# Turning nine of x's quantized tiles on VectorE inside the attention units, with GpSimd taking low parts

## The chip, the cores and the metric

The kernel runs on one core of a Trainium2 chip. The metric is the device time of one execution in microseconds (us): the median of the runs. A profiled execution has a span, from the first to the last instruction of the core, and a time of its own a little above it; the runs have no trace.

Engine names in the rows: PE is TensorE's matmuls, PEld its weight loads, DVE is VectorE, ACT is ScalarE, POOL is GpSimd, SPq the queue from which SyncE issues transfers. ps is PSUM.

## The reference, cut to what matters

The sizes are B = 4, T = 512, D = 512, 32 heads of 16, one key and one value head shared by all heads, and a feed-forward block of 2048 features.

```python
xn = layernorm(x)
s = attention(xn, wq, wk, wv, wo)        # causal; k and v are shared by the 32 heads
h = linear8bit(xn, W1, b1)
g = silu(linear8bit(h, W2, b2))
out = x + s * g

def linear8bit(x, W, b):
    col_max = max(abs(x)) over all rows
    outlier = col_max > 3.0
    y = quant_rows(where(outlier, 0, x)) @ quant_rows(W).T
    return y + where(outlier, x, 0) @ W.T + b
```

quant_rows rounds each row to multiples of its largest absolute value / 127.

## The kernel before, in words

The 2048 rows of x are 16 tiles of 128 rows. The kernel has three stages. The first normalizes x, stores it to DRAM and makes queries, keys and values. The second is attention. The third is the feed-forward block, whose first layer multiplies W1 by the quantized x, which has to lie in SBUF turned: the feature on the partition, the token along the row. Two big tensors hold it, big_h (the part that TensorE's fast format keeps) and big_l (what is left). Until then the same two tensors hold the queries and then the attended rows: tile i of x may be written only once the rows of tile i have been projected.

**Attention** runs over 16 units (4 batches by 4 groups of 8 heads). A unit has 24 steps, and all engines run the same list of steps `g`, each with its own part of each step in a fixed order. Parts that belong to different units are shifted against each other (the exponentials of a unit run 35 steps behind the start of its maxima). In a step there are, on PE: one piece of the raw scores for the row maxima (`max_piece`, L1010, into one of three PSUM banks `MAXB`), one piece of the final scores (L1023, three banks), in some steps the product with the values (`pv`, L1036) or one k of a row tile's output projection (L1061 to L1063: three matmuls, four k for each of 16 row tiles). On VectorE: the maximum of the piece (L933), which frees its bank; PE may not write piece n before the maximum of piece n - 3 is taken. In some steps there are also transposes and reciprocals of the normalization (L900 to L914) and the quantization of one tile of x (L723, L727, L731, L734). On ScalarE: the exponential (L854), the high part of the attended rows (L859), evictions (L715, L871) and the last step of quantization (L864). On GpSimd: the causal mask after some exponentials (L836), the inlier product and the rounding for x (L804, L809) and the low part of the attended rows (L825). SyncE's queue stores the quantized tile `xm` to `xe_scratch` in DRAM (L763, one transfer of 128 rows of 2 KB), loads the next normalized tile (L759), the queries of a later unit (L161, 12 transfers of 64 KB) and the maxima (L749), and stores projected rows (L789). GpSimd's product for tile u + 1 overwrites `xm` and waits for the store of tile u (`s_xes`).

Counted within a unit (g modulo 24), GpSimd has a mask in steps 1, 5, 7, 8, 14, 18, 20 and 21 and the product L804 in step 2. Of the products with the values, the one that uses the masks of steps 1 and 5 stands in step 9.

**The turned x before.** The first 12 tiles (`EARLY`) are turned once the last maximum piece is done (g = 384): every second step from g = 385 on, PE transposes a tile loaded back from DRAM (four 128 by 128 transposes with the identity, L1097, into a bank of `MAXB`), a step later ScalarE copies the high part into big_h (L881), and a step later VectorE subtracts to get the low part (L947). The loads (L769) go through two buffers and wait for the transposes two tiles back. In the same steps stand the exponentials, masks and value products of the last two units and the projection of the third batch's last three row tiles. The projection of the fourth batch follows at g = 423, and the feed-forward stage after that. The last four tiles are turned there and are not touched.

## Time and profile before

| | |
|---|---|
| median of 3 runs | 789.14 us (788.95 to 1225.57) |
| the profiled execution: its time | 788.52 us |
| its span | 786.8 us |
| mean granted TensorE clock | 0.984 |
| busy: PE, DVE, ACT, POOL | 752.1 (96%), 651.5 (83%), 396.0 (50%), 273.6 us (35%) |
| attention's steps g = 0 to 383, until | 364.1 us of the span |
| first matmul of the feed-forward stage | 409.09 us |
| a step block of 24 without projection / with it | 17.5 / 18.28 us |

Busy time of PE is that of matmuls with modelled ends: they are pipelined, so that one of 512 columns lasts 0.39 us and the next starts 0.23 us after it. A row of a timeline gives start and duration, both in us, then engine, line and operation, output and inputs, and how many such instructions are merged in it. The distance from one start to the next is what an instruction takes from its engine when it is kept busy.

The 24-step blocks can be told by L936, which ends each of them on VectorE: at 163.44, 180.94, 199.56, 217.84, 236.12, 254.40, 272.68, 290.97, 309.25, 327.54, 345.82 and 364.10 us. Blocks are numbered from 0 by g // 24; block 10 begins at 254.4 us.

### The profile page before, as it was taken

What the parts mean: (1) busy time and instruction counts of PE and PEld (TensorE: products, weight loads), DVE (VectorE), ACT (ScalarE), POOL (GpSimd) and SP (SyncE); (2) the same over time, 40 slices, a digit from 0 to 9 for tenths busy, and PEclk for the clock granted to TensorE, in tenths of its full rate; (3) what the DMA queues carried; (4) which work ended last, traced back from release to release, by engine and by line L of the source; (5) the groups of instructions that cost most, each with busy time, mean ns of one, the idle gap of its engine ahead of it and who ended that gap; (6) DMA issues with size and microseconds to landing.
All of it is one profiled execution on the core that took longest, in us unless ns stands there. A gap on an engine that the chain in (4) does not pass through costs nothing. (4 is left out here: it accounts for less than half of the span.)

```text
span 786.8 us, 11983 instructions
## 1 busy us (share of the span) xinstructions
PE 752.1 (96%) x4133; PEld 567.0 (72%) x4133; DVE 651.5 (83%) x1116; ACT 396.0 (50%) x671; POOL 273.6 (35%) x349
## 2 busy tenths in 40 slices
PE   5999899999999999999999999999997999999995
PEld 4877575556666677666568878878886888888884
DVE  7988989999989999987447668597859998599957
ACT  4454066676777677667824445355554333132212
POOL 7213135555555555555442112122100000027404
PEclk9999689999999999999999999999999999999998
DMA  7431302332333332233455677646334678427982
GB/s 261 157 108 54 78 21 70 86 83 76 91 91 105 89 83 84 83 83 122 135 192 185 166 237 197 202 105 161 88 62 131 240 241 255 157 87 245 332 278 107
DMA packets 93772, 110.71 MB, mean 141 GB/s; under 512 B 43136, under 2 KB 50320, under 8 KB 92176
## 3 DMA queue, kind: packets, MB, share of 16 engines
q1 hardware_dynamic: 93712, 109.95, 45.8%
q8 instruction: 33, 0.54, 0.3%
q14 instruction: 27, 0.22, 0.1%
HBM read 56.43 MB, written 40.37 MB: 123 GB/s over the span
## 5 line engine op out<-in xcount | busy, mean ns | idle before, releaser
L933 DVE TENSOR_REDUCE rowmax<-ps 128x2 f32<-128x512 f32 (+3 forms) x384 | 210.7, 590 | 20.3 <-PE ps L1010 18.7
L854 ACT ACTIVATE probs<-ps 128x512 f32<-128x512 f32 (+1 forms) x352 | 175.3, 557 | 72.0 <-PE ps L1023 70.3
L1010 PE MATMUL ps<-km,stack 128*128 128x256 f32 (+3 forms) x512 | 150.2, 347 | 2.6 <-PEq L195 1.9
L1023 PE MATMUL ps<-stack,ks 128*128 128x512 f32 (+1 forms) x352 | 132.8, 387 | 2.7 <-ACT probs L854 2.7
L1010 PEld LDWEIGHTS ps<-km,stack 128*128 128x128 f32 (+1 forms) x512 | 95.1, 199 | 43.1 <-DVE rowmax L933 23.5
L836 POOL TENSOR_SCALAR_AFFINE_SELECT probs<-probs 128x512 f32<-128x512 f32 x128 | 81.0, 641 | 78.9 <-ACT probs L854 77.3
L1880 PE MATMUL ps<-big_h 128*128 128x512 f32 x256 | 100.0, 390 | 2.0 <-DVE big_l L1696 1.6
L1881 PE MATMUL ps<-big_l,big_h 128*128 128x512 f32 x256 | 99.6, 389 | 0.0
L1882 PE MATMUL ps<-big_h,big_l 128*128 128x512 f32 x256 | 99.6, 389 | 0.0
L1036 PE MATMUL ps<-probs,vones 128*32 128x512 f32 (+3 forms) x1024 | 82.2, 439 | 0.2 <-POOL probs L836 0.2
L1023 PEld LDWEIGHTS ps<-stack,ks 128*128 128x128 f32 x352 | 67.4, 192 | 11.7 <-ACT probs L854 6.2
L1880 PEld LDWEIGHTS ps<-big_h 128*128 128x128 f32 x256 | 48.0, 188 | 12.6 <-issue 2.6
L1036 PEld LDWEIGHTS ps<-probs,vones 128*32 128x32 f32 x1024 | 26.7, 109 | 41.2 <-issue 28.1
L1882 PEld LDWEIGHTS ps<-big_h,big_l 128*128 128x128 f32 x256 | 48.1, 188 | 10.1
L1881 PEld LDWEIGHTS ps<-big_l,big_h 128*128 128x128 f32 x256 | 48.1, 188 | 9.7
L1625 DVE TENSOR_TENSOR absmax<-absmax,habs 128x2048 f32<-128x2048 f32 x15 | 34.3, 2285 | 22.0 <-ACT habs L1265 22.0
L1857 PE MATMUL ps<-big_h,w_high_first 128*128 128x512 f32 x128 | 50.8, 397 | 1.6 <-PEq L708 1.6
L1857 PE MATMUL ps<-big_h,w_high_second 128*128 128x512 f32 x128 | 50.7, 396 | 1.4 <-POOL w_low_second L1427 1.4
L1546 ACT CAST big_h<-habs 128x1024 fp32r<-128x1024 f32 x31 | 32.4, 1045 | 39.0 <-DVE habs L1668 23.3
L1859 PE MATMUL ps<-big_h,w_low_second 128*128 128x512 f32 x128 | 50.5, 395 | 0.0
L1859 PE MATMUL ps<-big_h,w_low_first 128*128 128x512 f32 x128 | 50.5, 395 | 0.0
L1858 PE MATMUL ps<-big_l,w_high_first 128*128 128x512 f32 x128 | 50.5, 395 | 0.0
(227 smaller groups left out, 1370.0 us busy)
## 6 DMA issues: line engine op xcount, KB each, us to landing
stack<-big_h SPq DMA_DIRECT2D x128, 64.0 KB, 2.0
h_scratch<-hs SPq DMA_DIRECT2D x7, 1024.0 KB, 4.7
hload<-h_scratch SPq DMA_DIRECT2D x14, 512.0 KB, 5.2
xn_scratch<-xa SPq DMA_DIRECT2D x4, 1024.0 KB, 4.4
stack<-big_l SPq DMA_DIRECT2D x64, 64.0 KB, 2.0
xi<-xn_scratch SPq DMA_DIRECT2D x16, 256.0 KB, 2.7
xe_scratch<-xm SPq DMA_DIRECT2D x16, 256.0 KB, 2.3
w2n<-in_L_ffn_W_dram SPq DMA_DIRECT2D x4, 1024.0 KB, 6.5
```

What stands on the lines that cost most here:

```text
L836: nc.gpsimd.affine_select(out=d, in_=d, compare_op=ALU.is_ge, fill=0.0, base=0, pattern=[[0, NPAIR], [1, P]], channel_multiplier=-1).then_ ...
L854: nc.scalar.activation(probs[p][:, o:o + nh * w], ps[:, STB[n % NST], 0:nh * w], ACT.Exp).then_inc(s_exp, 1)
L933: nc.vector.tensor_reduce(dst, src, AX_X, ALU.max).then_inc(s_red, 1)
L1010: last = nc.tensor.matmul(dst, stack[u % 3][rows, hp, P * qt:P * (qt + 1)], km[rows, u // KT, p0:p0 + npar, keys], start=True, stop=True)
L1023: ins = nc.tensor.matmul(ps[:, STB[n % NST], 0:nh * w].rearrange("p (h q) -> p h q", h=nh), ks[:, u // KT, p, P * kt:P * (kt + 1)], stack[ ...
L1036: ins = nc.tensor.matmul(ps[32 * j:32 * j + 32, PVB, P * kt:T], vones[:, u // KT, kt, :], probs[p][:, o:o + w], start=(kt == 0), stop=(kt ...
L1857: nc.tensor.matmul(dst, w1h[f % 2][:, k, :], big_h[:, k, t], start=(k == 0), stop=False)
L1858: nc.tensor.matmul(dst, w1h[f % 2][:, k, :], big_l[:, k, t], start=False, stop=False)
L1859: last = nc.tensor.matmul(dst, w1l[f % 2][:, k, :], big_h[:, k, t], start=False, stop=(k == KT - 1))
L1880: nc.tensor.matmul(ps[:, i, :], hqh[m % RB][:, t], w2h[m % RB], start=(kk == 0), stop=False)
L1881: nc.tensor.matmul(ps[:, i, :], hqh[m % RB][:, t], w2l[m % RB], start=False, stop=False)
L1882: return nc.tensor.matmul(ps[:, i, :], hql[m % RB][:, t], w2h[m % RB], start=False, stop=(kk == FT - 1))
```

## The change

Nine tiles (0 to 8, `STEADY`) are turned within the blocks 7 to 15, one in each, in step 2 of the block; tiles 9, 10 and 11 at g = 386, 394 and 402. VectorE turns a tile in SBUF, in blocks of 32 by 32, with one instruction. For that to be the whole transpose, the first 12 tiles are stored to DRAM with their 32 by 32 blocks exchanged: four transfers of 32 partitions each, whose pieces in DRAM are 32 elements (128 bytes). The load back is issued 19 steps before the turn, in step 7 of the block before, and it comes into `tail_rows[:, 0]`; the turned tile stands in `tail_rows[:, 1]`. One step after the turn ScalarE copies it to big_h, now from SBUF, and two steps after it GpSimd (not VectorE) subtracts for big_l. PE's 48 transposes are gone. The next turn on VectorE waits for GpSimd's subtraction of the tile before. The wait for big_l's 12 tiles and for the last maximum moves to the projection of the fourth batch.

```diff
         EARLY = NT - QT
-        TAIL_STEP = 2
+        def x_stores(n):
+            return 16 * (HB * min(n, EARLY) + max(n - EARLY, 0))
         W1_LOAD_AT, W1_SCALE_AT, W1_ROUND_AT = 21, 30, 31
         W2_LOAD_AT, W2_SCALE_AT = 28, 38
         W1_TURN_AT, W1_HIGH_AT, W1_LOW_AT = 36, 37, 37
...
         def projected_rows(i):
             return tail_rows[:, i % 2, :] if i in TAIL_OUT else ob[:, i % 2, :]
-        def tail_tile(g, after=0):
-            i, r = divmod(g - after - CH * U - 1, TAIL_STEP)
-            return i if r == 0 and 0 <= i < EARLY else -1
+        TURN_AT, STEADY = 2, 9
+        def turned(g, after=0):
+            t = g - after
+            if t < CH * U:
+                i = t // CH - KT - 3
+                return i if t % CH == TURN_AT and 0 <= i < STEADY else -1
+            i, r = divmod(t - CH * U - TURN_AT, 8)
+            return STEADY + i if r == 0 and i < EARLY - STEADY else -1
+        def x_fetched(g):
+            i = turned(g, 5 - CH)
+            if 0 <= i <= STEADY:
+                return i
+            i = turned(g, -6)
+            return i if i > STEADY else -1
         misc = []
         for g in range(STEPS):
...
                     u = unit_at(g, XSTORE_AT)
                     if u >= 0:
                         sp.wait_ge(s_xe, u + 1)
-                        sp.dma_start(xe_d[P * u:P * (u + 1), :], xm[:, :]).then_inc(s_xes, 16)
-                    i = tail_tile(g, -5)
+                        if u < EARLY:
+                            for b in range(HB):
+                                sp.dma_start(xe_d[P * u:P * (u + 1), :]
+                                             .rearrange("(a j) (k b i) -> b j k a i", a=HB, k=KT, b=HB)[b],
+                                             xm[SQ * b:SQ * (b + 1), :].rearrange("j (k a i) -> j k a i", k=KT, a=HB)
+                                             ).then_inc(s_xes, 16)
+                        else:
+                            sp.dma_start(xe_d[P * u:P * (u + 1), :], xm[:, :]).then_inc(s_xes, 16)
+                    i = x_fetched(g)
                     if i >= 0:
-                        sp.wait_ge(s_xes, 16 * (i + 1))
-                        if i >= 2:
-                            sp.wait_ge(s_tt, i - 1)
-                        sp.dma_start(tail_rows[:, i % 2, :], xe_d[P * i:P * (i + 1), :]).then_inc(s_tr[i % 2], 16)
+                        sp.wait_ge(s_xes, x_stores(i + 1))
+                        if i:
+                            sp.wait_ge(s_tt, i)
+                        sp.dma_start(tail_rows[:, 0, :], xe_d[P * i:P * (i + 1), :]).then_inc(s_tr, 16)
                     if unit_at(g, XSTORE_AT + 1) == U - 1:
                         sp.wait_ge(s_xm, NT)
-                        sp.wait_ge(s_xes, 16 * (EARLY + 1))
+                        sp.wait_ge(s_xes, x_stores(EARLY + 1))
                         sp.dma_start(inlier_row[:, :], xe_d[P * EARLY:P * (EARLY + 1), :]).then_inc(s_xel[0], 16)
                     if unit_at(g, W1_LOAD_AT) == U - 1:
                         sp.wait_ge(s_xt, NT)
...
                     if u >= 0:
                         pool.wait_ge(s_xl, 16 * (u + 1))
                         if u:
-                            pool.wait_ge(s_xes, 16 * u)
+                            pool.wait_ge(s_xes, x_stores(u))
                         nc.gpsimd.tensor_tensor(xm[:, :], xi[:, :], inlier_row[:, :],
                                                 ALU.mult).then_inc(s_xm, 1)
                     u = unit_at(g, XROUND_AT)
...
                         pool.wait_ge(s_ah, u + 1)
                         nc.gpsimd.tensor_tensor(attended(big_l, u), tb[:, :, :].rearrange("p a b -> p (a b)"),
                                                 attended(big_h, u).bitcast(F32), ALU.subtract).then_inc(s_al, 1)
+                    i = turned(g, 2)
+                    if i >= 0:
+                        pool.wait_ge(s_xh, i + 1)
+                        nc.gpsimd.tensor_tensor(big_l[:, :, P * i:P * (i + 1)],
+                                                tail_rows[:, 1, :].rearrange("p (k t) -> p k t", k=KT),
+                                                big_h[:, :, P * i:P * (i + 1)].bitcast(F32),
+                                                ALU.subtract).then_inc(s_xlo, 1)
                     u, s_ = scored(g)
                     p, i = divmod(s_, NB)
                     if u >= 0 and s_ < 2 * NB and i + 1 in KT_END:
...
                     b, j, k = projected(g, 1)
                     if b >= 0 and k == KT - 1:
                         evict(act, b, j)
-                    i = tail_tile(g, 1)
+                    i = turned(g, 1)
                     if i >= 0:
+                        act.wait_ge(s_mf, misc_at[("o", *divmod(i, QT))] + 1)
                         act.wait_ge(s_tt, i + 1)
                         nc.scalar.copy(big_h[:, :, P * i:P * (i + 1)],
-                                       ps[:, MAXB[i % NMAX], :].rearrange("p (k t) -> p k t", k=KT)).then_inc(s_xh, 1)
+                                       tail_rows[:, 1, :].rearrange("p (k t) -> p k t", k=KT)).then_inc(s_xh, 1)
             @block.vector
             def _(dve):
...
                     for part in range(4):
                         if unit_at(g, XSCALE_AT + part) >= 0:
                             quantize_x(dve, unit_at(g, XSCALE_AT + part), part)
-                    i = tail_tile(g, 2)
+                    i = turned(g)
                     if i >= 0:
-                        dve.wait_ge(s_xh, i + 1)
-                        nc.vector.tensor_tensor(big_l[:, :, P * i:P * (i + 1)],
-                                                ps[:, MAXB[i % NMAX], :].rearrange("p (k t) -> p k t", k=KT),
-                                                big_h[:, :, P * i:P * (i + 1)].bitcast(F32),
-                                                ALU.subtract).then_inc(s_xlo, 1)
+                        dve.wait_ge(s_tr, 16 * (i + 1))
+                        if i:
+                            dve.wait_ge(s_xlo, i)
+                        nc.vector.transpose(tail_rows[:, 1, :], tail_rows[:, 0, :]).then_inc(s_tt, 1)
                     if unit_at(g, W1_SCALE_AT) == U - 1:
                         dve.wait_ge(s_w1n[0], 16)
...
                     if k == 0:
                         misc_bank(("o", b, j))
                         if b == B - 1 and j == 1:
+                            pe.wait_ge(s_red, CH * U)
                             pe.wait_ge(s_xlo, EARLY)
                     pe.wait_ge(s_al, KT * b + k + 1)
                     c = slice(P * j, P * (j + 1))
...
                         maxima(maximized(g, MAX_AT))
                     if projected(g)[0] >= 0:
                         project(*projected(g))
-                    i = tail_tile(g)
-                    if i >= 0:
-                        pe.wait_ge(s_tr[i % 2], 16 * (i // 2 + 1))
-                        if i < NMAX:
-                            pe.wait_ge(s_red, CH * U)
-                        else:
-                            pe.wait_ge(s_xlo, i - NMAX + 1)
-                        for k in range(KT):
-                            last = nc.tensor.transpose(ps[:, MAXB[i % NMAX], P * k:P * (k + 1)],
-                                                       tail_rows[:, i % 2, P * k:P * (k + 1)], ident[:, :])
-                        last.then_inc(s_tt, 1)
                     if unit_at(g, W1_TURN_AT) == U - 1:
                         pe.wait_ge(s_w1r, 1)
                         pe.wait_ge(s_exp, 2 * NB * U)
```

## Rows read from the trace of the kernel before

**Rows 1.** Page, part 1: busy us, share of the span, instructions of each engine.
```profile
PE 752.1 (96%) x4133; PEld 567.0 (72%) x4133; DVE 651.5 (83%) x1116; ACT 396.0 (50%) x671; POOL 273.6 (35%) x349
```

**Rows 2.** Windows: two blocks and the stretch after the last; per engine busy (count).
```profile
146.40:163.90 17.50, 16.88 (x123) 10.24 (x122) 16.86 (x37) 12.14 (x26) 9.92 (x14) 1.00 0.29 79
218.00:236.30 18.30, 18.30 (x136) 12.67 (x135) 16.78 (x38) 12.92 (x28) 10.00 (x14) 1.00 0.32 89
364.30:409.10 44.80, 40.38 (x270) 26.81 (x270) 21.87 (x40) 28.00 (x56) 19.92 (x25) 1.00 0.44 144
```

**Rows 3.** Timeline of DVE in block 10 (one answer per narrow window).
```profile
255.28 3.27 DVE L933 TENSOR_REDUCE rowmax<-ps 128x2 f32<-128x512 f32 x6
...
256.48 0.68 DVE L933 TENSOR_REDUCE rowmax<-ps 128x4 f32<-128x512 f32 x1
257.19 0.56 DVE L933 TENSOR_REDUCE rowmax<-ps 128x1 f32<-128x384 f32 x1
...
262.09 0.56 DVE L933 TENSOR_REDUCE rowmax<-ps 128x1 f32<-128x384 f32 x1 [0.50 <-PE ps L1010]
...
269.50 0.70 DVE L914 STREAM_TRANSPOSE tb<-ta 128x512 f32<-128x512 f32 x1
270.13 0.65 DVE L933 TENSOR_REDUCE rowmax<-ps 128x4 f32<-128x512 f32 x1
```

**Rows 4.** Timeline of PE in block 10.
```profile
257.17 0.34 PE L1010 MATMUL ps<-km,stack 96*128 96x384 f32 x1
...
257.52 0.28 PE L1010 MATMUL ps<-km,stack 128*128 128x256 f32 x1
...
257.87 0.44 PE L1010 MATMUL ps<-km,stack 96*128 96x256 f32 x2
...
259.97 1.71 PE L1036 MATMUL ps<-probs,vones 128*32 128x512 f32 x16
```

**Rows 5.** Timelines of DVE and of PE in an earlier block, without projection.
```profile
141.50 0.43 DVE L933 TENSOR_REDUCE rowmax<-ps 128x2 f32<-128x256 f32 x1
141.98 0.39 PE L1010 MATMUL ps<-km,stack 128*128 128x256 f32 x1
```

**Rows 6.** Timelines of POOL and of the SP queue in block 10.
```profile
257.43 1.30 POOL L804 TENSOR_TENSOR xm<-xi,inlier_row 128x512 f32<-128x512 f32 x1 [1.10 <-DMA xe_scratch<-xm]
258.77 0.64 POOL L836 TENSOR_SCALAR_AFFINE_SELECT probs<-probs 128x512 f32<-128x512 f32 x1
...
253.48 0.58 SPq L763 DMA_DIRECT2D xe_scratch<-xm  x1
```

**Rows 7.** Stores of a like shape: page, part 6, and line L1304 (duration ns min/median/max).
```profile
w2t_scratch<-w2e SPq DMA_DIRECT2D x64, 64.0 KB, 2.0
L1304 SPq DMA_DIRECT2D w2t_scratch<-w2e x64: 303/503/1292, 426.4 to 575.3; - x64
```

**Rows 8.** PE's transposes: lines (busy, mean ns), timeline, and a wait of 364:409.
```profile
L1097 PE MATMUL ps<-ident,tail_rows 128*128 128x128 f32 x48 | 7.4, 278 | 0.8 <-DMA tail_rows<-xe_scratch 0.7
...
370.87 0.60 PE L1097 MATMUL ps<-ident,tail_rows 128*128 128x128 f32 x4
371.22 0.47 PE L1023 MATMUL ps<-stack,ks 128*128 128x512 f32 x1
...
PE ps L1097 <- DMA tail_rows<-xe_scratch: 0.7, 1, 0.7
```

**Rows 9.** Timelines of ACT, POOL and PE near the end of the last unit.
```profile
385.94 0.63 ACT L859 CAST big_h<-tb 128x512 fp32r<-128x512 f32 x1
...
386.65 1.29 POOL L825 TENSOR_TENSOR big_l<-tb,big_h 128x512 fp32r<-128x512 f32 x1 [2.87 <-ACT big_h L859]
387.88 1.23 POOL L836 TENSOR_SCALAR_AFFINE_SELECT probs<-probs 128x512 f32<-128x512 f32 x2
390.91 0.64 POOL L836 TENSOR_SCALAR_AFFINE_SELECT probs<-probs 128x512 f32<-128x512 f32 x1 [1.79 <-ACT probs L854]
...
390.29 0.86 PE L1036 MATMUL ps<-probs,vones 128*32 128x256 f32 x16
```

More of the change, by code:

```diff
@@ L551, in block_layernorm_attention_ffn @@
         rec = sa("rec", [P, 2, T // 32])
+        HB, SQ = 4, 32
         def attended(part, u):
@@ L607, in block_layernorm_attention_ffn @@
         s_nm = sem("heads_divided")
-        s_tr = [sem(f"tail_rows_loaded{i}") for i in range(2)]
-        s_tt = sem("tail_rows_transposed")
+        s_tr = sem("x_blocks_loaded")
+        s_tt = sem("x_blocks_turned")
         s_w1n = [sem(f"w1_loaded{i}") for i in range(2)]
@@ L790, in _ @@
                                      ).then_inc(s_obt if n in TAIL_OUT else s_obs[n % 2], 16)
-                sp.wait_ge(s_xes, 16 * NT)
+                sp.wait_ge(s_xes, x_stores(NT))
             @block.gpsimd
@@ L1154, in block_layernorm_attention_ffn @@
         s_t2 = sem("absmax_transposed")
-        HB, SQ = 4, 32
         def w2_pieces(f):
```

## The prediction

> **What bounds the kernel now.** I read the page's busy shares first, then the windows by block, then the timelines of single blocks, last the stretch after g = 383. PE is busy 96% of the span [rows 1]; the reader should not stop there, because the change touches only the attention stage. There two kinds of block are to be told apart. Without projection a block takes 17.5 us, with 16.88 us of PE and 16.86 of DVE [rows 2]: PE and DVE take turns at waiting for each other. With projection it takes 18.28 us, PE is busy throughout and DVE 16.78 [rows 2]. So the blocks in which the nine turns are put are bound by PE, and DVE has about 1.5 us left in each. That room is an average. What counts is where in the block it lies, since PE may not write a piece before DVE has taken the maximum three pieces back. After the last block follow 44.8 us in which PE is busy 40.38 [rows 2], with the 48 transposes among them.
>
> **The blocks: the turn on DVE.** No row shows this instruction, but L914 is the same operation on the same shape from SBUF to SBUF: it lasts 0.70 us, and the next maximum starts 0.63 us after it [rows 3]. I take 0.63; below, an idle engine would make it 0, above, 0.70. It comes behind the third maximum. In block 10 the maxima of steps 1 to 6 stand without a gap to speak of [rows 3]; that of step 3 starts at 256.48 and ends at 257.16, that of step 4 starts at 257.19, some 0.1 us later than it could, since it waits for PE. With the turn the one ends at 257.79 and the other, with 0.53 of delay left, at 257.75 + 0.53 = 258.28.
> PE's piece of step 6 needs the first of these, that of step 7 the second. They start now at 257.52 and 257.87 [rows 4]. How soon PE follows a maximum is seen in an earlier block: a maximum ends at 141.93 and PE's piece starts at 141.98 [rows 5]. So step 6 starts at 257.84 (0.32 late) and step 7 at 258.33, 0.46 late, and 0.45 is what I take. The piece of step 10 isn't late on DVE's account: before its maximum DVE idles 0.50 us [rows 3], which swallows the 0.53. From there DVE is again where PE puts it. Nothing gives PE's 0.45 us back, since it has no idle time in such a block. It has the same margins in each of blocks 7 to 15: 9 x 0.45 = **+4.05 us**. Bounds: 9 x 0 if the piece of step 7 isn't really held, and 9 x 0.70 = 6.3 if the whole turn lands on PE.
>
> **The blocks: what stands beside.** ScalarE's copy waits for the turn to end at 257.18; it and what is behind it (the exponential of step 4, the eviction L871, then PE's projection) come about 0.4 us late, no later than PE. It is free while PE sets the pace; without PE's delay it would cost the same 0.4, not in addition. The load back is a unit ahead and costs one issue on a queue that waits in that place.
> The store becomes four transfers of 64 KB in pieces of 128 bytes. The same shape is stored at L1304: 0.50 us of issue, 2.0 from issue to landing [rows 7]. Issued from 253.48 on [rows 6], 0.54 apart, the last lands at 253.48 + 1.62 + 2.0 = 257.1. GpSimd's product L804 waits for it and starts now at 257.43, released by the single store [rows 6]; so nothing gets later. The three more issues (1.6 us) push the store of projected rows back, and SP waits idle after that.
> GpSimd's subtraction costs 1.29 us (L825, the same operation [rows 9]). It comes behind L804, and behind it are the masks of steps 5, 7 and 8. L804 ends at 258.7, the subtraction at 259.95, the mask of step 5 at 260.6. PE's value product starts at 259.97 [rows 4] and reaches the half that needs this mask about 0.9 later, 261.3 with PE's own delay. Margin 0.7 us: I cost it at nothing, and its price if the cover is gone is the time by which L804 starts after 258.2.
> The Trainium skill (DMA: Bandwidth & Descriptors, Why small descriptors are slow) speaks against such a store: each packet carries a fixed 3 cycles over its 32-byte beats, 7 instead of 4 for 128 bytes. L1304's transfers agree in so far as 64 KB land in 2.0 us: the cost is there but below a microsecond. By the rule alone the sum would stay, as long as the last transfer lands by 258.2.
>
> **The stretch after the blocks.** PE loses twelve groups of four transposes. Four start at 370.87 and the next matmul at 371.22 [rows 8]: 0.35 us, 0.35 to 0.42 over the twelve, together 4.5. The wait for a loaded tile, 0.7 [rows 8], goes too: 5.2 us at most. Two things stand in the way. One group (g = 395) lies in the shadow of an eviction that PE waits for, 0.36 lost. The larger is GpSimd, which must now do tile 11's subtraction in g = 404, behind L825 and ahead of the masks of g = 404 and 405. L825 follows ScalarE's L859, 385.94 [rows 9]. Up to there ScalarE gains 1.9 us from the five groups before g = 394 and, from g = 395 on, three copies fewer at 0.5 (five of the old go, two of the new come): 3.4, less the shadowed 0.36, so L825 starts at 386.65 - 3.05 = 383.6. It ends at 384.8, the subtraction at 386.05, the masks at 386.65 and 387.25. PE has its value product of g = 411 at 390.29 [rows 9]; it could start at 385.2 but its second half waits for the last mask until 387.3, where it began at 390.7: 3.4 us earlier instead of 5.1. After that the masks at 390.91 and later [rows 9] come 3.7 earlier and set the last value products. I take **-3.7 us**, bounds -3.0 and -5.2. The projection and the start of the feed-forward stage shift with it, and that stage is PE's own: nothing there is bought or lost.
>
> **The sum**, against the profiled 788.52: + 4.05 - 3.7 = 788.9. The median of the runs lies 0.6 above the profiled time; a part of that I add: **789.3 us**.
>
> **The rivals.**
> *A, the forecast*: the turn costs PE what DVE lacks, the stretch returns it. 787 to 791.5. Chance 0.55.
> *C, the turns are absorbed*: PE isn't held in steps 6 and 7, and the 1.5 us of DVE's room cover 0.63. For it: DVE's idle share. Against it: the margins at 257.52 and 257.87 are 0.36 and 0.13 us. It gives 788.5 - 3.7 + 0.5 = 785.3. Chance 0.17.
> *B, GpSimd's queue becomes the bound in the blocks*, the case on the slower side: the last of the four stores lands late, L804 starts after 258.2, the subtraction stands before the mask of step 5, and PE waits for it in step 9. For it: the single store of block 10 took 3.95 us to release L804 (253.48 to 257.43 [rows 6]), twice what L1304's take. A last landing 4.0 after its issue (259.1) costs 0.9 in each of the 8 blocks 7 to 14: 789.3 + 7.2 = 796.5. Against it: today the store of projected rows is issued right behind and shares the engines, in future only after. Chance 0.24, of it 0.03 that the store lands 2.0 us beyond the threshold or more, from where on it decides over 2% (8 x 2.0 = 16).
> *D, the transposes count in full*, so that moving them is worth more than their distance: 7.4 us busy [rows 8] and the wait 0.7, minus 4.05, gives 785.1, and with C 781. Against it: they overlap. Chance 0.04.
> Under the rule of the Trainium skill (VectorE: DVE Perf Modes, The three transpose paths) a 128 by 128 transpose costs TensorE 390 ns, 48 of them 18.7 us, so by it D would give some 774; the trace has four in 0.35 us, which is against it.
>
> **How the numbers follow.** The likeliest case is A. The range takes in C at its low end and the lower half of B: 785.0 to 795.0; outside are the rest of B (0.11) and most of D (0.04) and some of C (0.03). About 2%, 15.8 us, is what a measurement of this kernel can tell from no change. Faster by that much takes more than C and D together: 0.01. Slower needs B beyond its threshold: 0.03. Within 2%: 0.96.
>
> **What would show it.** Blocks 7 to 15 of 18.7 us instead of 18.28, with the whole difference between PE's pieces of steps 5 and 8, prove the DVE step right; 18.3 proves C. PE waiting for L836 in step 9, with L804 released by the store, is B. In the stretch, PE waiting at the value product of g = 411 for a mask behind the new subtraction supports -3.7; if the feed-forward stage starts 5 us earlier after block 15's end than now, the GpSimd step was wrong. The prediction falls if stores of 128 bytes behave otherwise beside 12 query loads than L1304's, or if the exponentials of ScalarE, not GpSimd, set the stretch.

## The result and the profile after

| | before | after |
|---|---|---|
| median, 8 runs each | 789.3 us (788.7 to 1225.57) | 794.87 us (791.02 to 797.05) |
| ratio of the two | | 1.0068 [1.0047, 1.009] |
| profiled execution: its time, its span | 788.52, 786.8 | 791.02, 789.2 |
| blocks 7 to 15 in the profile | 164.5 | 171.4 |
| end of block 15 to the feed-forward stage | 45.0 | 41.7 |

One execution of before lies at 1225.57 us, far from all others, and plays no part. The forecast was 789.3, with a range of 785.0 to 795.0; the change costs 0.7%. The profiled execution is the lowest of the eight, so what it shows is the least that the change did.

What follows rests on the lengths of the blocks, from one start of the block-ending maximum to the next. Before, each of blocks 7 to 15 takes 18.28 us. After:

```
block       7      8      9      10     11     12     13     14     15
after     18.72  18.70  18.70  19.57  19.01  19.49  19.28  19.20  18.69
```

Two levels are to be seen: 18.7 in four blocks, and up to 0.9 more in the five from 10 to 14. The sum is 6.8 us more than before; the stretch after the blocks gives 3.3 back, what lies ahead of block 7 is 1.6 shorter in this execution and the feed-forward stage 0.4 longer: 6.8 - 3.3 - 1.6 + 0.4 = 2.3, and the spans differ by 2.4. The last two are no effect of the change that the runs show: in the traces of this document the part ahead of block 7 takes 196.9 to 199.6 us (199.6 in before, 197.9 in a run with the same code up to there), and the feed-forward stage 377.7 to 379.7, once 382.1.

The changed kernel's page, part 1: busy us, share of the span, instructions.

```profile
PE 749.4 (95%) x4085; PEld 560.3 (71%) x4085; DVE 649.0 (82%) x1116; ACT 396.1 (50%) x671; POOL 288.6 (37%) x361
```

Beside [rows 1], PE has its 48 transposes less, and GpSimd twelve subtractions more, 15.0 us. PE is no longer busy throughout in the blocks. Its waits by releaser over 180 to 412 us (sum, count, longest):

```profile
PE ps L1070 <- POOL probs L870: 3.1, 5, 1.3
PE ps L1044 <- DVE rowmax L968: 1.9, 9, 0.2
```

L870 is what L836 was (the mask), L968 what L933 was (the maximum), L1044 and L1070 are the pieces and the value product, L831 is the product that was L804. Nine waits for a maximum, one for each of the nine blocks; of the five for a mask, the longest lies in the stretch and four in the blocks (in block 11, the fifth that loses time, it is PE's weight load that waits for the mask). The timeline of DVE in block 10 of after, which begins at 254.10 (first columns start and duration), and then that of PE:

```profile
254.97 1.28 DVE L968 TENSOR_REDUCE rowmax<-ps 128x2 f32<-128x512 f32 x2
256.17 0.70 DVE L984 STREAM_TRANSPOSE tail_rows<-tail_rows 128x512 f32<-128x512 f32 x1
256.80 1.91 DVE L968 TENSOR_REDUCE rowmax<-ps 128x4 f32<-128x512 f32 x4
```

```profile
257.05 0.33 PE L1057 MATMUL ps<-stack,ks 128*128 128x384 f32 x1
257.59 0.36 PE L1044 MATMUL ps<-km,stack 128*128 128x256 f32 x1 [0.21 <-DVE rowmax L968]
...
258.02 0.45 PE L1044 MATMUL ps<-km,stack 96*128 96x256 f32 x2
...
260.07 1.06 PE L1070 MATMUL ps<-probs,vones 128*32 128x512 f32 x8
261.79 0.85 PE L1070 MATMUL ps<-probs,vones 128*32 128x384 f32 x8 [0.65 <-POOL probs L870]
```

The turn takes its engine for 0.63 us. Counted from the start of the block, PE's piece of step 6 starts at 3.49 instead of 3.12 [rows 4], that of step 7 at 3.92 instead of 3.47: 0.37 and 0.45 late, where 0.32 and 0.46 were forecast. Then the value product comes in two parts with a hole of 0.65 us between them (0.86 by the starts, since eight take 0.86 and the second part starts 1.72 after the first), where before all 16 ran together [rows 4]. That hole is the second level. GpSimd's timeline, and the issues of SP's queue in the same block:

```profile
258.59 1.31 POOL L831 TENSOR_TENSOR xm<-xi,inlier_row 128x512 f32<-128x512 f32 x1 [2.57 <-DMA xe_scratch<-xm]
259.85 1.30 POOL L857 TENSOR_TENSOR big_l<-tail_rows,big_h 128x512 fp32r<-128x512 f32 x1
261.08 1.83 POOL L870 TENSOR_SCALAR_AFFINE_SELECT probs<-probs 128x512 f32<-128x512 f32 x3
```

```profile
253.69 3.17 SPq L785 DMA_DIRECT2D xe_scratch<-xm  x4
```

The chain is complete in these four rows: the four stores take 3.2 us of SP's queue, GpSimd waits 2.57 us for the last to land, starts L831 at 258.59, does the new subtraction behind it, and only then the mask for which PE stands still. Block 8, where nothing is lost, and block 14, where 0.5 is:

```profile
215.84 2.65 SPq L785 DMA_DIRECT2D xe_scratch<-xm  x4
...
331.20 2.63 SPq L785 DMA_DIRECT2D xe_scratch<-xm  x4
```

These last as long as each other, but the first begins 0.86 before its block (216.70) and the second 0.25 before (331.45). For all nine blocks, in us from the start of the block: the issue of the first and of the last of the four, the start of L831, and by how much the block is over 18.7 (block 15 has one plain store):

```
block       7     8     9     10    11    12    13    14    15
first     -0.86 -0.86 -0.87 -0.41 -0.87  0.00 -0.34 -0.25  0.28
last       1.14  1.15  1.13  2.12  1.55  2.01  1.67  1.76   -
L831      3.51  3.52  3.51  4.49  3.95  4.44  4.22  4.13  2.70
over 18.7  0     0     0    0.87  0.31  0.79  0.58  0.50   0
```

In each of the five the loss is the start of L831 less 3.62 to 3.65; the prediction put that point at 258.2 - 254.4 = 3.8. And L831 follows the last issue by 2.37 in five of the eight blocks with four stores, by 2.40 to 2.56 in the others. So the landing is steady; what varies is when the last issue happens: either the whole row begins late, behind the query loads of the same queue (blocks 12 to 14), or a single store in it takes long (block 11), or both (block 10).

In the stretch, the timelines of GpSimd and PE (block 15 ends at 369.34):

```profile
388.93 1.27 POOL L852 TENSOR_TENSOR big_l<-tb,big_h 128x512 fp32r<-128x512 f32 x1 [2.69 <-ACT big_h L893]
390.17 1.27 POOL L857 TENSOR_TENSOR big_l<-tail_rows,big_h 128x512 fp32r<-128x512 f32 x1
391.39 1.80 POOL L870 TENSOR_SCALAR_AFFINE_SELECT probs<-probs 128x512 f32<-128x512 f32 x3
```

```profile
392.07 1.01 PE L1070 MATMUL ps<-probs,vones 128*32 128x256 f32 x16 [1.26 <-POOL probs L870]
```

PE does wait for the masks behind tile 11's subtraction. Its value product starts 22.73 us after block 15, against 26.19 before [rows 9]: 3.46 us earlier. The 3.3 us of the stretch are one draw: the five other traces in which GpSimd subtracts tiles 9 to 11 have 41.6 to 42.7 us there, so it gave 2.3 to 3.4.

### The profile page after: what moved, and what is told of

Its sections match the earlier page's. It is cut to its first block and busy times, and to the rows that moved or that the text cites. A ratio compares the mean times of both kernels' runs of the same rounds, so it can differ in the third digit from the quotient of the medians.

```text
span 789.2 us, 11946 instructions
## 1 busy us (share of the span) xinstructions
PE 749.4 (95%) x4085; PEld 560.3 (71%) x4085; DVE 649.0 (82%) x1116; ACT 396.1 (50%) x671; POOL 288.6 (37%) x361
## 5 line engine op out<-in xcount | busy, mean ns | idle before, releaser
L968 DVE TENSOR_REDUCE rowmax<-ps 128x2 f32<-128x512 f32 (+3 forms) x384 | 210.3, 590 | 22.7 <-PE ps L1044 21.2
L1044 PE MATMUL ps<-km,stack 128*128 128x256 f32 (+3 forms) x512 | 150.6, 347 | 4.6 <-DVE rowmax L968 2.4
L1044 PEld LDWEIGHTS ps<-km,stack 128*128 128x128 f32 (+1 forms) x512 | 94.1, 197 | 48.4 <-DVE rowmax L968 23.1
L870 POOL TENSOR_SCALAR_AFFINE_SELECT probs<-probs 128x512 f32<-128x512 f32 x128 | 80.0, 642 | 54.0 <-ACT probs L888 53.9
L1070 PE MATMUL ps<-probs,vones 128*32 128x512 f32 (+3 forms) x1024 | 83.5, 439 | 3.4 <-POOL probs L870 3.1
L1070 PEld LDWEIGHTS ps<-probs,vones 128*32 128x32 f32 x1024 | 26.0, 109 | 46.7 <-issue 24.7
L1880 PE MATMUL ps<-big_l,w_high_second 128*128 128x512 f32 x128 | 50.5, 395 | 0.0
```

The source lines that it names most:

```text
L870: nc.gpsimd.affine_select(out=d, in_=d, compare_op=ALU.is_ge, fill=0.0, base=0, pattern=[[0, NPAIR], [1, P]], channel_multiplier=-1).then_ ...
L968: nc.vector.tensor_reduce(dst, src, AX_X, ALU.max).then_inc(s_red, 1)
L1044: last = nc.tensor.matmul(dst, stack[u % 3][rows, hp, P * qt:P * (qt + 1)], km[rows, u // KT, p0:p0 + npar, keys], start=True, stop=True)
L1070: ins = nc.tensor.matmul(ps[32 * j:32 * j + 32, PVB, P * kt:T], vones[:, u // KT, kt, :], probs[p][:, o:o + w], start=(kt == 0), stop=(kt ...
L1880: nc.tensor.matmul(dst, w1h[f % 2][:, k, :], big_l[:, k, t], start=False, stop=False)
```

## The experiments

The theory after the result is that two separate costs add up, 0.42 us in each of nine blocks from the turn on VectorE and the rest from the stores in four parts, through GpSimd. The first two experiments undo the second cost in two ways, the third brings in the first cost by itself. The median of before is given anew with each experiment, 788.1 to 788.9 us; a ratio is always to the before beside it.

**The store in one part.** It leaves out the exchange of the 32 by 32 blocks.

```diff
-            return 16 * (HB * min(n, EARLY) + max(n - EARLY, 0))
+            return 16 * n
...
-                        if u < EARLY:
+                        if u < 0:
```

> The changed kernel, but each of the first 12 tiles is stored with the one transfer of 2 KB rows again, so x's blocks lie in the wrong order (that part of the result is left out). Theory (PE loses 0.43 us per block to the turn, and in blocks 10 to 14 another 0.3 to 0.85 because the last of four stores releases GpSimd's product L804 late and its subtraction then stands before the mask that PE needs): blocks 7 to 15 all take 18.7 us, GpSimd's product starts 1.9 to 3.0 us into a block, no value product waits for a mask; 791.0 - 3.0 = 788 us, ratio to before about 0.999. Rival (the subtraction on GpSimd costs this by itself, whatever the store does): blocks 10 to 14 stay at 19.0 to 19.6, ratio 1.007. Rival (the traffic of loads back disturbs): as the second.

Measured: 789.26 us, 1.0002 [0.9985, 1.0019] of before (788.88). All nine blocks take 18.7, together 3.8 us more than before. GpSimd's timeline in its block 10, from 255.17 on:

```profile
257.49 1.29 POOL L831 TENSOR_TENSOR xm<-xi,inlier_row 128x512 f32<-128x512 f32 x1 [0.40 <-DMA xe_scratch<-xm]
258.75 1.29 POOL L857 TENSOR_TENSOR big_l<-tail_rows,big_h 128x512 fp32r<-128x512 f32 x1
```

L831 starts 2.3 after the block instead of 4.5, and PE waits for no mask in the blocks. The second level is gone, the first has stayed.

**The subtraction behind the masks** (in step 9 of the block instead of step 4; tiles 9 to 11 as they were). The stores stay in four parts.

```diff
                     # GpSimd, ahead of the subtraction of the nine tiles
-                    i = turned(g, 2)
+                    i = turned(g, 7)
... (for tiles 9 to 11 turned(g, 2), as it was)
```

> The changed kernel, with GpSimd's nine subtractions of the blocks moved from step 4 to step 9, behind the masks of steps 5, 7 and 8. Theory: the store may land as late as now, but nothing that PE needs stands behind the subtraction: blocks 7 to 15 take 18.7 us, ratio about 0.999. Rival (a late L804 alone delays the mask of step 5 and VectorE's L723): blocks 10 to 14 stay over 18.9, ratio 1.003 or more.

Measured: 789.2 us, 0.9998 [0.9984, 1.0012]. Blocks of 18.68 to 18.73. GpSimd in block 10 (from 254.64):

```profile
259.46 1.30 POOL L831 TENSOR_TENSOR xm<-xi,inlier_row 128x512 f32<-128x512 f32 x1 [2.89 <-DMA xe_scratch<-xm]
260.69 1.82 POOL L874 TENSOR_SCALAR_AFFINE_SELECT probs<-probs 128x512 f32<-128x512 f32 x3
262.47 1.30 POOL L861 TENSOR_TENSOR big_l<-tail_rows,big_h 128x512 fp32r<-128x512 f32 x1
```

Here the product starts 4.8 after the block, later than in any block of after, and nothing is lost. So a late store alone costs nothing, and the subtraction ahead of the masks alone costs nothing (previous run); only both together do.

**The turn alone, in the kernel before.** Nine turns of a row that is there anyway; nothing else of the change.

```diff
+                    if g < CH * U and g % CH == 2 and g // CH >= 7:
+                        nc.vector.transpose(tail_rows[:, 1, :], magic_row[:, :])
```

> The kernel before with nine more 128x512 transposes on VectorE in step 2 of blocks 7 to 15 (from a constant row into a buffer that nobody reads there), nothing else. Theory: each delays PE's pieces of steps 6 and 7 and costs 0.43 us, blocks 7 to 15 at 18.7, all of them alike: 789.3 + 3.9 = 793.2 us, ratio 1.005. Rival (the cost of blocks 7 to 9 comes from ScalarE's copy ahead of the exponential and the eviction): 18.28 us a block, ratio 1.000.

Measured: 792.93 us against 788.88, +4.05 us, 1.0048 [1.003, 1.0067]. Blocks of 18.64 to 18.69, 3.44 together. DVE and PE in block 8 (216.31 to 234.99), then the block as a window (length; PE, PEld, DVE, ACT and POOL busy; clock; DMA share; GB/s):

```profile
218.67 0.70 DVE L945 STREAM_TRANSPOSE tail_rows<-magic_row 128x512 f32<-128x512 f32 x1
...
220.09 0.36 PE L1012 MATMUL ps<-km,stack 128*128 128x256 f32 x1 [0.24 <-DVE rowmax L933]
...
216.31:234.99 18.68, 18.44 (x135) 12.61 (x135) 17.25 (x38) 12.89 (x27) 9.98 (x14) 1.00 0.31 87
```

The same wait of PE at the same piece as in after: of the 0.42 us a block of the first level, 0.38 are the turn on VectorE by itself. Where the other 0.04 come from isn't shown; ScalarE's copy is one candidate. DVE is idle for 1.4 of 18.7 us in this block, and that does not help: its idle time lies elsewhere in the block.

**The turn in another place.** In step 22 of the block before DVE waits for PE ahead of a maximum. Only the turn and what counts from it move.

```diff
-                i = t // CH - KT - 3
-                return i if t % CH == TURN_AT and 0 <= i < STEADY else -1
+                i = t // CH - KT - 2
+                return i if t % CH == BLOCK_TURN_AT and 0 <= i < STEADY else -1   # 22
```

> The changed kernel, with the nine turns in step 22 of the block before instead of step 2 (the copy in step 23, the subtraction in step 0). VectorE idles 0.85 us there today, and GpSimd is idle before the mask of step 1. Theory: both costs go, the blocks with a turn take 18.3 us, and with the 3.3 us that the stretch after the blocks gives the kernel takes 785.5 to 786.5, ratio 0.996. Rival (the turn costs PE 0.4 us wherever it stands, as DVE has no room): 18.7 us a block, ratio 0.999 to 1.001.

Measured: 790.13 us, 1.0014 [1.0001, 1.0026], blocks of 18.75 to 18.79: no better than in step 2, and the theory of this run failed. DVE around the turn, then ScalarE and PE:

```profile
215.78 0.69 DVE L984 STREAM_TRANSPOSE tail_rows<-tail_rows 128x512 f32<-128x512 f32 x1
216.72 0.56 DVE L968 TENSOR_REDUCE rowmax<-ps 128x1 f32<-128x384 f32 x1 [0.25 <-PE ps L1044]
...
217.45 0.61 ACT L916 CAST big_h<-tail_rows 128x512 fp32r<-128x512 f32 x1
217.96 1.85 ACT L888 ACTIVATE probs<-ps 128x512 f32<-128x512 f32 x4
...
218.61 0.44 PE L1057 MATMUL ps<-stack,ks 128*128 128x384 f32 x1 [0.22 <-ACT probs L888]
```

The turn itself became free: after it DVE still waits 0.25 for PE. But ScalarE's copy moved with it, to step 23, where the exponentials are not ahead of PE: they come 0.5 late and PE waits for one. A new wait took the place of the old one. The next run gives every part its own place.

**Three parts, three idle places.** As in the last run, with ScalarE's copy in step 9 and GpSimd's subtraction in step 10 of the next block.

```diff
+        def behind(g, in_block, later):
+            i = turned(g, in_block)
+            if 0 <= i < STEADY:
+                return i
+            i = turned(g, later)
+            return i if i >= STEADY else -1
...
-                    i = turned(g, 2)        # GpSimd's subtraction
+                    i = behind(g, 12, 2)
...
-                    i = turned(g, 1)        # ScalarE's copy
+                    i = behind(g, 11, 1)
```

> The changed kernel with the nine turns in step 22 of the block before, as in the run with step 22, but ScalarE's copy in step 9 and GpSimd's subtraction in step 10 of the block after the turn, where each of them idles. In the run with step 22 alone VectorE's maxima were as before and PE waited in step 3 for an exponential that stood behind the copy. Theory (the cost is whichever engine's order the part stands in, not the work): blocks 6 to 15 at 18.3 us, against 18.77; with 3.3 us from the stretch after the blocks the kernel takes 785.5 to 786 (ratio 0.996). Rival (the blocks have no room for the three parts at all): 18.6 or more.

Measured: 785.95 us against 788.9, 0.9963 [0.995, 0.9977]. Blocks: 18.28 to 18.32 in seven of nine, 18.45 and 18.48 in blocks 12 and 14; +0.4 in all. A block as a window (columns as above):

```profile
216.59:234.87 18.28, 18.28 (x136) 12.66 (x135) 17.37 (x38) 13.40 (x28) 11.15 (x15) 1.00 0.43 103
```

DVE is busy 17.37 us in it, more than in after (17.24 in block 8), and the block has before's length. Two blocks still lose 0.2: there the product on GpSimd starts 4.6 and 4.7 after the block, lasts 1.3, and delays the mask of step 5 to 5.9 without any subtraction between.

**The later tiles, too.** As above, and the subtractions of tiles 9, 10 and 11 by VectorE again.

```diff
                     # GpSimd
-                    if i >= 0:
+                    if 0 <= i < STEADY:
...
                     # VectorE, ahead of the turn
+                    i = turned(g, 2)
+                    if i >= STEADY:
+                        dve.wait_ge(s_xh, i + 1)
+                        nc.vector.tensor_tensor(big_l[...], tail_rows[:, 1, :], big_h[...], ALU.subtract)
```

> The run before this one, and tiles 9, 10 and 11 are subtracted by VectorE two steps after their turn instead of by GpSimd. Theory (in the stretch after the blocks PE waits 1.3 us for masks that stand behind GpSimd's subtraction of tile 11): that wait goes, the stretch shrinks from 41.7 to about 40.4 us, total 784.5, ratio 0.994. Rival (ScalarE's exponentials set that stretch, and the mask is late only as far as they are): the stretch keeps 41.5 us.

Measured: 785.68 us, 0.9953 [0.9935, 0.997]. The stretch takes 40.38 us instead of 42.1, and its GpSimd and PE show why:

```profile
383.91 1.28 POOL L860 TENSOR_TENSOR big_l<-tb,big_h 128x512 fp32r<-128x512 f32 x1 [2.68 <-ACT big_h L901]
385.14 1.80 POOL L878 TENSOR_SCALAR_AFFINE_SELECT probs<-probs 128x512 f32<-128x512 f32 x3
...
385.82 1.01 PE L1085 MATMUL ps<-probs,vones 128*32 128x256 f32 x16
```

The masks follow L860 at once, and PE's product has no wait. Yet the median is only 0.3 below the run before and 1.2 above the 784.5 of the theory. In the profiled execution the span is even 0.3 longer than in the run before: of the 1.8 us gained, 0.4 is given back in blocks with late stores, 0.7 ahead of block 7 and 1.0 in a longer feed-forward stage (378.9 against 377.9). This run by itself does not prove that the gain in the stretch reaches the end.

**The turn in step 2 once more,** copy in step 3, subtraction in step 9, VectorE's subtractions for tiles 9 to 11: against the last run only the places in the blocks differ, those of the turn, of the copy and of the subtraction.

> The changed kernel with the nine subtractions in step 9 as in the run with that alone, and tiles 9, 10 and 11 subtracted by VectorE. Blocks 7 to 15 stay at 18.70 us. Theory: the stretch takes about 40.3 us against 41.6, ratio 0.998. Rival: 41.5 us, ratio 1.000.

Measured: 787.54 us, 0.9989 [0.9976, 1.0002], blocks of 18.70, 3.8 together against 0.8 in the last run, stretch 40.38 again. Moving the three parts to their idle places is worth 3.0 us in the blocks and 1.9 in the medians.

**Ten tiles in the blocks** instead of nine (`STEADY = 10`; tiles 10 and 11 stay at g = 394 and 402), otherwise as in the last but one.

> As the run with free slots and VectorE's subtractions, but tile 9 too is turned in step 22 of block 15, tiles 10 and 11 after the blocks. Theory: PE does not transpose either of them, so one tile more or less in the stretch changes nothing that sets its end: within 0.3 us of that run. Rival (each tile in the stretch costs ScalarE 0.5 us there, and ScalarE sets it): 0.5 us less.

Measured: 785.83 us, 0.9951 [0.9931, 0.9972], stretch 40.39. The tenth tile moves nothing: once no mask waits behind a subtraction, no tile in the stretch is in PE's way. What PE still waits for there are exponentials, two evictions (1.03 and 0.94 us) and the start of the feed-forward stage (1.62). In this execution block 10 took 19.14 and block 11 18.75; in them GpSimd's product starts 5.32 and 4.94 after the block, behind stores of which the first took 2 us to issue. So the improved places don't do away with the late store; the last two runs do.

**The changed kernel again, and two stores.** Three runs are left: the changed kernel itself once more, then the improved one (places as above, nine tiles, VectorE's subtractions) with the store in one part, which again leaves out the exchange, and last the improved one with the four stores in another place of SP's queue, behind the first six query loads of a later unit instead of behind all twelve.

> The changed kernel as it is, once more. Theory (the last of four stores lands at a time that differs from execution to execution, and where it is late PE waits for the mask behind GpSimd's subtraction): blocks 7 to 9 again 18.70, blocks 10 to 14 again between 18.9 and 20, but not the same numbers as in the first profile; total between 791 and 797. Rival (the loss of blocks 10 to 14 belongs to something fixed in the program): the same block lengths to 0.1 us.

Measured: 794.36 us against 788.14, 1.0081 [1.0064, 1.0099]. Its blocks sum to 9.3 us over before, after's to 6.8; blocks 8 and 10 are the long ones now (19.83 and 20.33). The stores of its block 10 (from 254.21) and GpSimd behind them, then the same of block 8 (from 215.64):

```profile
253.91 3.87 SPq L785 DMA_DIRECT2D xe_scratch<-xm  x4
...
259.52 1.29 POOL L831 TENSOR_TENSOR xm<-xi,inlier_row 128x512 f32<-128x512 f32 x1 [3.38 <-DMA xe_scratch<-xm]
...
214.78 2.63 SPq L785 DMA_DIRECT2D xe_scratch<-xm  x4
...
220.46 1.29 POOL L831 TENSOR_TENSOR xm<-xi,inlier_row 128x512 f32<-128x512 f32 x1 [2.89 <-DMA xe_scratch<-xm]
```

In block 10 one store took 1.85 us to issue, and L831 follows the last issue by the usual 2.37. In block 8 the issues were early and short, and for once the landing was late: 3.68 after the last issue. The expectation failed in these two blocks (8 was to stay at 18.70, 10 below 20).

Nor is all of the loss a matter of chance. Over 18.7, blocks 12 to 14 lose 0.85, 0.51 and 0.51 here and 0.79, 0.58 and 0.50 in after, the same to 0.1 us, as the rival said. Of the four stores in block 10 one is long in both (after, then this run), and the same query load ahead of block 14 is:

```profile
254.35 1.15 SPq L785 DMA_DIRECT2D xe_scratch<-xm  x1
326.77 1.22 SPq L161 DMA_DIRECT2D stack<-big_h  x1
...
253.91 1.85 SPq L785 DMA_DIRECT2D xe_scratch<-xm  x1
328.12 1.31 SPq L161 DMA_DIRECT2D stack<-big_h  x1
```

Counted in the order of SP's issues over the whole trace, this holds for all nine traces with four stores (632 issues each): in the blocks from 10 on there are six places, the 205th or 206th issue, the 225th to 227th, the 243rd or 244th, the 260th to 263rd, the 279th and the 293rd or 294th, and in 51 of the 54 cases the issue there takes 0.97 to 2.04 us. With the stores in their old place, the first two places fall on the four stores of blocks 10 and 11 and the others on query loads ahead of blocks 12 to 15; in blocks 7 to 9 only the run with the stores between the query loads (the last one below) has issues of such a length, two of them. So the place is nearly fixed by the order of the queue, and what changes between executions is the length, most of all in blocks 10 and 11.

> The run with free slots and VectorE's subtractions after the blocks, but with one plain transfer for each stored tile (x's blocks in the wrong order, that part of the result is left out). Theory: what blocks 10, 12 and 13 of that run lost (18.45 to 18.57) is the late landing of four stores: all blocks 7 to 15 at 18.28 to 18.3, 0.7 us less in all, ratio 0.994. Rival (the loads back or the subtraction cause it): unchanged.

Measured: 784.34 us, 0.995 [0.9936, 0.9964]; all nine blocks 18.28 to 18.31. The 0.2 to 0.3 left in single blocks was the store's.

```diff
                     # SP, in the step of the query loads
-                        queries(u + 3)
+                        queries(u + 3, range(0, 2))
+                        store_x(u)
+                        queries(u + 3, range(2, NPAIR))
... (the old place keeps the stores of the last three units alone)
```

> The run with free slots and VectorE's subtractions, correct in full, with the four stores of a tile issued between the first six and the last six loads of the queries instead of behind all twelve. Theory: the last store then lands before the next block begins, GpSimd's product L831 starts 1.9 us into every block and no longer when the store allows, blocks 7 to 15 at 18.28, ratio 0.994. Rival (the later six loads of queries come too late for PE, or the queue waits for ScalarE's last step of quantization): 18.5 or more.

Measured: 783.6 us (783.3 to 784.76), 0.9943 [0.9929, 0.9958]. SP in block 9, and GpSimd in block 10 (from 252.74):

```profile
248.29 2.64 SPq L777 DMA_DIRECT2D xe_scratch<-xm  x4
...
254.02 0.64 POOL L883 TENSOR_SCALAR_AFFINE_SELECT probs<-probs 128x512 f32<-128x512 f32 x1 [0.58 <-ACT probs L901]
254.62 1.28 POOL L844 TENSOR_TENSOR xm<-xi,inlier_row 128x512 f32<-128x512 f32 x1
```

The product starts 1.9 after the block in every block and waits for nothing; blocks of 18.28 to 18.33. The long issues stand at the same places of the queue, but now the stores have time for them: the 205th issue is a query load now (1.54 us at 252.29), and where a store is the long one (the 279th, 1.61 us, block 14) the product still starts at 1.9. This version computes everything and is faster than both kernels: 4.5 us below the before beside it, some 11 below after. Against the version with late stores (0.9953) its profile has 0.7 us less in the blocks; the intervals of the two ratios overlap, so the medians alone don't show that step.

## Why the prediction was right and wrong

**The turn on DVE: right, in size and place.** +4.05 was forecast (0.45 a block), and 3.8 are in the blocks of the runs without the second cost (0.42 a block); the turn alone in the kernel before costs 3.4 in the blocks and 4.05 in the median. It came from following two maxima to the two pieces that wait for them. The share of idle time (rival C) would have given nothing; C is refuted by the blocks of 18.7.

**The stretch: right in its cause, a little too large.** -3.7 was forecast, -3.3 measured in after and -2.3 to -3.4 over the six traces with this code, against a bound of -3.0; the cause is the named one: the value product of g = 411 waits for a mask behind tile 11's subtraction and starts 3.46 us earlier (forecast 3.4). L852 follows block 15 by 19.59; the prediction had 383.6 - 364.1 = 19.5. With the subtraction on VectorE the stretch takes 40.38, 4.6 less than before. Rival D is refuted as well: the most that the stretch returned is 4.6, not 8.1. (The 390 ns for one transpose in the prediction are the figure of the Trainium skill, VectorE: DVE Perf Modes, The three transpose paths, for bf16; the transposes here are fp32, and [rows 8] has four in 0.35 us.)

**The store: the step that failed.** "Issued from 253.48 on [rows 6], 0.54 apart, the last lands at 253.48 + 1.62 + 2.0 = 257.1 ... so nothing gets later." The term was put at nothing and cost 3.05 us in the profiled execution, 5 to 6 by the medians. The mechanism was that of rival B; two terms of this sum were too small and one was read in one block only. Line L785 of after (duration ns min/median/max):

```profile
L785 SPq DMA_DIRECT2D xe_scratch<-xm x48: 616/629/1154, 126.6 to 333.2; - x48
...
DMA to landing us min/median/max: 2.2/2.2/3.2
```

First, the sizes: an issue takes 0.63, not 0.50 [rows 7], the next follows at 0.67, and GpSimd follows the last issue by 2.37, not 2.0. That makes 3 x 0.67 + 2.37 = 4.38 instead of 3.62. From 0.92 before the block, as in block 10 of before, L831 starts at 3.46: still ahead of the threshold, and just what blocks 7 to 9 show (3.51, nothing lost). The margin was 0.2, not 0.7.

Second, the place: 253.48 was taken from block 10 and applied to all. The trace of before has the store as early as that in blocks 7 to 11 alone; in blocks 12 to 14 it is issued 0.44, 0.70 and 0.17 before the block. SP's queue in before ahead of block 14 (327.54), and GpSimd behind it:

```profile
322.80 1.35 SPq L161 DMA_DIRECT2D stack<-big_h  x1
...
327.36 0.58 SPq L763 DMA_DIRECT2D xe_scratch<-xm  x1
...
329.81 1.29 POOL L804 TENSOR_TENSOR xm<-xi,inlier_row 128x512 f32<-128x512 f32 x1 [0.35 <-DMA xe_scratch<-xm]
```

One of the twelve query loads took 1.35 us to issue instead of 0.59, and the store behind them was late by as much. Before, that cost nothing; with 4.38 behind it, -0.17 becomes 4.21 and 0.58 us of loss (0.50 measured in after). By this way the three blocks give 0.3, 0.05 and 0.6, about 1 us together that could be read in the trace of before. Block 11 could be read too: right behind its single store the next issue, of projected rows, takes 1.11 us there. With one of the four stores in that place the sum is -0.92 + 4.38 + 0.48 = 3.94, a loss of 0.3, and 0.31 is measured. Block 10 has no long issue in before, but 1.04 to 2.12 us at this place in the three other traces with single stores; its 0.87, and how long each long issue gets, no single trace could give. The prediction had the spread in its rows, 303 to 1292 ns [rows 7] and the 3.95 us of the single store [rows 6], and held its margin against the median.

**The sum.** By the medians, the changed kernel without the second cost is at 789.2 (subtraction moved) and 789.26 (store in one part), which is the forecast of 789.3; the second cost is the 5 to 6 us that are left. B came on top of A, as its price of 796.5 had it, in five of the eight blocks and not in all. The most likely case, A with 787 to 791.5, did not come. That 794.87 lies within the range is owed to the half of B that was taken into it, and by 0.13 us to luck: four of the eight executions lie above 795.0. The 0.4 us added for median over profile were too little, 3.85 measured, for the same reason: where a cost depends on how long a queue's issues get, one profile is a draw. That after's other seven executions, up to 797.05, lose their time in the same place is inferred from the second profile of the program (2.5 us more in the blocks, span 2.2 longer); they were not traced. The two runs in which the store can cost nothing have their profiled time near or above the median (789.3 to 789.2, 790.59 to 789.26).

**The small packets.** The Trainium skill (DMA: Bandwidth & Descriptors, Why small descriptors are slow) speaks of a fixed cost for each small packet in the engines. The landing of 64 KB in 128-byte pieces at 2.2 us agrees in so far as that cost can't be more than a part of 2.2 us. No run here shows the cost itself, so the prediction's "the cost is there" was not read from a row: the plain store of 256 KB landed in 2.3 us. What the four stores added was time in the issuing queue, three more issues, 3 x 0.67 = 2.0 us.

## What to carry to other kernels

- An instruction moved to another engine is costed at its place in that engine's order, by following its successors to the first one on which the bound engine waits; the same three parts cost 0.42 us a block in one set of places, 0.5 in another and nothing in a third, where VectorE was no less busy. Every part needs its own place: when the copy moved along behind the turn, one wait was only exchanged for another.
- A margin behind a DMA is to be held against the latest issue of all its instances, not one, and against the upper end of the row. Long issues are to be looked for by their place in the queue: a transfer that is put in such a place, or behind it, takes the delay over. Four transfers for one add three issues to the queue; the cure was to issue them earlier, between other transfers of the same queue.

## What the runs showed of the hardware

- An issue of 64 KB in 512 pieces of 128 bytes takes SP's queue 0.63 us (0.616 to 0.64 in nearly all), but single issues on that queue, query loads as well as stores, take 0.97 to 2.04. In the nine traces with four stores they come in blocks 10 to 15 at nearly the same six places in the order of the queue, whatever transfer stands there, 14 to 21 issues apart. What makes them long stayed open.
- The landing behind such an issue was steadier than the issue: in the 64 blocks with four stores in the old place and a product that waits for them, L831 (or what stands for it) followed the last issue by 2.36 to 2.64 us in 63, by 3.68 in one.
- VectorE's turn of 128x512 took its engine for 0.63 us in after too, and the sum of row durations gave PE's delay behind it to 0.05 us: 0.32 and 0.46 forecast, 0.37 and 0.45 measured.
